# Routed experts on gathered token tiles instead of on every token, in a one-core attention and mixture-of-experts kernel

## The chip, the cores and the metric

The kernel runs on one core of one Trainium2 chip. The metric is device microseconds of one launch; the kernel before takes 1021.36 us (median of 3 runs, 1020.69 to 1021.43).

## What is computed

The input x is 8 sequences of 256 tokens with H = 256 (2048 tokens). A first block (normalised attention with quantised projections, self and cross, 16 heads of 128) adds its output to x. The change touches the second block only:

```python
x = x + tanh(g_ffn[0]) * ffn(_layernorm(x))

def _moe_forward(hidden_states, gate_w, w1, w3, w2, sw1, sw3, sw2):   # T 2048, E 8, I 176, K 2
    scores = softmax(x @ gate_w.T)
    topk_w, topk_idx = top_k(scores, K)
    topk_w = topk_w / sum(topk_w)
    h = einsum('th,ehi->eti', x, w1)
    g = einsum('th,ehi->eti', x, w3)
    y_all = einsum('eti,eih->eth', silu(h) * g, w2)
    y = sum(y_all[topk_idx, tok] * topk_w)
    shared = silu(x @ sw1) * (x @ sw3) @ sw2                          # width 352
    return y + shared
```

## The kernel before, in words

Each engine has its own program, written out by hand, and semaphores join them: `done(engine, s, n)` waits until counter s has passed n. The attention stage is 64 steps (8 sequences by 8 groups) in a software pipeline that is six steps deep; `tick(b, g)` on each engine issues that engine's share of up to six steps. `tick(B, g)` for g = 0 to 4 drains it and already does the first steps of the second block. Step `tick(B, 4)` ends with the last output projection (L456, into the PSUM bank JB). `residual` (L992) adds the last sequence to xs, `tail1` takes its statistics, POOL's `tail` (L1366) normalises it into zf, PE turns it (L337), and ACT and DVE write it as two fp16 halves, `tail_high` (L641) and `tail_low` (L954), into zT_hi and zT_lo. All matrix products of the second block are three matmuls (`split3`, L319: high by high, high by low, low by high).

The second block treats the 8 experts and the shared expert as one hidden width of 1760 for all tokens. It goes over 4 blocks of 512 tokens, and in each over 14 chunks of 128 hidden columns (the last has 96): `ffn_up` (L527) is 2 by 6 matmuls of 512 columns, `ffn_down` (L556) 12 matmuls of 256 columns, and for the 11 chunks of experts `weigh` (L602) spreads the routing weight of each token over the rows by one matmul into the bank VB, so that an expert that a token did not choose counts zero. ACT takes the silu (L870) and the high half (L865), DVE the product (L1302), the weight (L1307) and the sum into the output (`finish`, L1284), and POOL the low half (L1458). The chunks of block 0 are written out and overlap with the rest of the routing, the weights' halves (`ffn_high` on ACT, L660, `ffn_low` on DVE, L986, 7 units of two chunks, each loaded by SP) and the last sequence's normalisation; blocks 1 to 3 run as a loop. The routing itself is `logits` on PE, `read_logits`, `best` and `weights` on DVE (L1238 to L1278), in two portions: the first 14 tiles of 128 tokens, and the last sequence's two.

SP issues the loads, the transposes of the attention (`flip`) and the stores. POOL issues one DMA (wp, L1438). `JB`, `VB`, `A0`, `A1`, `S0`, `S1`, `T0`, `T1` are the 8 PSUM banks; the profile leaves the numbers out.

## Time and profile before

| | |
|---|---|
| median of 3 runs | 1021.36 us |
| the profiled execution's own time | 1020.03 us |
| its span, first to last instruction | 1018.3 us |
| PE busy | 930.3 us (91%), 6752 matmuls |
| DVE, ACT busy | 760.0 us, 759.8 us (75% each) |
| POOL busy | 704.2 us (69%) |
| granted TensorE clock, mean | 0.973 |
| DMA | 63.12 MB, 62 GB/s |
| chain that ended last | PE 59%, issue 16%, DVE 10%, POOL 6%, ACT 5% |

A busy share is of the whole span. Matmuls are pipelined: the time of one in a timeline is longer than the distance to the next, and the distance is what counts where they follow each other. The granted clock is 1.00 at 2.4 GHz and 0.50 at 1.2 GHz.

### The profile page before, as it was taken

The numbers are of one execution on the slowest core, as the hardware profiler recorded it, in microseconds if no ns is written. First come the engines' busy times: TensorE is split into PE (matmuls) and PEld (weight loads), VectorE is DVE, ScalarE is ACT, GpSimd is POOL, SyncE is SP. The second block draws the span as 40 slices with busy tenths as digits, with TensorE's granted clock in tenths as the row PEclk, the third lists the DMA queues.
The fourth block names the chain that finished last, engine by engine and source line by source line (L and its number), as shares of the span: only waits on it lengthen the run. The fifth ranks groups of instructions, "written<-read, shape, count | busy, mean of one in ns | idle before, by whom it ended". The sixth has DMA issues, their size and how long they took to land.

```text
span 1018.3 us, 21021 instructions
## 1 busy us (share of the span) xinstructions
PE 930.3 (91%) x6752; PEld 665.4 (65%) x6752; DVE 760.0 (75%) x1612; ACT 759.8 (75%) x2396; POOL 704.2 (69%) x533
## 2 busy tenths in 40 slices
PE   0375899999999999999999999999976999999998
PEld 0254677778787787778778777877733555555554
DVE  8899789888888988888988889898863833333332
ACT  3486899999999999999999999999873432222221
POOL 4597789799898888979988988888831422232322
PEclk9697899999999999999999999999997999999999
DMA  9323223333242333324233332423434100000000
GB/s 251 104 83 101 61 53 74 58 62 68 51 77 51 68 61 62 67 51 77 51 69 60 59 70 51 77 51 71 112 64 118 59 1 22 1 21 0 21 0 21
DMA packets 183265, 63.12 MB, mean 62 GB/s; under 512 B 167248, under 2 KB 180912, under 8 KB 183232
## 3 DMA queue, kind: packets, MB, share of 16 engines
q1 hardware_dynamic: 179120, 60.62, 27.3%
q0 software_dynamic: 4112, 2.10, 1.5%
q8 instruction: 17, 0.28, 0.1%
q14 instruction: 16, 0.13, 0.0%
HBM read 20.76 MB, written 2.10 MB: 22 GB/s over the span
## 4 chain that ended last, share of the span: by engine, by line
PE 59%; issue 16%; DVE 10%; POOL 6%; ACT 5%; DMA 1%; SPq 1%; POOLq 0%; DVEq 0%; ACTq 0%
PE S L426 10%; PE A L329 7%; PE A L330 7%; PE T L397 5%; POOL pT L1458 5%; PE JB L456 5%; PE S L414 4%; PE VB L321 3%; PE VB L323 2%; PE VB L322 2%; PE T L447 2%; DVE stage L977 1%; ACT zq L637 1%; DVE zq L935 1%; PE T L322 1%
## 5 line engine op out<-in xcount | busy, mean ns | idle before, releaser
L1346 POOL TENSOR_TENSOR rstd<-var,mhalf 128x8 f32<-128x8 f32 (+1 forms) x128 | 191.1, 1509 | 76.7 <-DVE var L1054 76.3
L329 PE MATMUL A<-w_hi,xq 128*128 128x256 f16 (+1 forms) x1024 | 187.4, 249 | 35.4 <-DVE v_lo L1028 20.5
L1458 POOL TENSOR_TENSOR pT<-zq,pT 128x512 f16<-128x512 f32 (+1 forms) x56 | 65.3, 1165 | 181.9 <-ACT pT L865 174.3
L330 PE MATMUL A<-w_lo,xq 128*128 128x256 f16 (+1 forms) x1024 | 187.4, 249 | 0.0
L426 PE MATMUL S<-kT,qT 128*128 128x256 f32 x512 | 142.1, 401 | 8.5 <-ACT kT L732 4.3
L870 ACT ACTIVATE qT<-A 128x512 f32<-128x512 f32 (+1 forms) x56 | 33.4, 596 | 152.2 <-PE A L323 152.2
L1040 DVE TENSOR_SCALAR qT<-T,qmap 128x512 f32<-128x512 f32 x128 | 103.6, 809 | 55.5 <-PE T L397 55.5
L1012 DVE TENSOR_REDUCE nmx<-S 128x2 f32<-128x512 f32 (+1 forms) x192 | 114.7, 598 | 28.0 <-PE S L426 25.6
L329 PEld LDWEIGHTS A<-w_hi,xq 128*128 128x128 f16 x1024 | 101.3, 99 | 47.0 <-issue 30.7
L743 ACT ACTIVATE prob<-S,nmx 128x256 f32<-128x256 f32 x256 | 119.3, 480 | 14.8 <-DVE nmx L1012 13.5
L1408 POOL TENSOR_TENSOR raw<-raw,rstd 128x1024 f32<-128x1024 f32 x64 | 126.3, 1974 | 0.0
L1392 POOL TENSOR_TENSOR prob<-prob,rl 128x1024 f32<-128x1024 f32 x64 | 120.9, 1889 | 0.0
L426 PEld LDWEIGHTS S<-kT,qT 128*128 128x128 f32 x512 | 89.9, 194 | 42.1 <-ACT kT L732 15.1
L330 PEld LDWEIGHTS A<-w_lo,xq 128*128 128x128 f16 x1024 | 101.3, 99 | 7.7
L1302 DVE SCALAR_TENSOR_TENSOR qT<-S,qT 128x512 f32<-128x512 f32 x44 | 30.4, 690 | 95.4 <-PE S L323 90.6
L698 ACT ACTIVATE raw<-A 128x512 f32<-128x512 f32 x128 | 80.1, 626 | 5.1 <-PE A L330 5.1
L751 ACT ACTIVATE probx<-S,nmx 128x64 f32<-128x64 f32 x256 | 77.7, 336 | 7.4 <-DVE nmx L1012 7.4
L1017 DVE SCALAR_TENSOR_TENSOR psrc<-prob,psrc 128x1024 f16<-128x1024 f32 x64 | 77.9, 1217 | 3.8 <-ACT psrc L767 3.8
L397 PE MATMUL T<-idt,raw 128*128 128x128 f32 x512 | 79.3, 278 | 1.0 <-ACT yb L776 1.0
L1045 DVE TENSOR_REDUCE ss<-sq 128x8 f32<-128x1024 f32 x64 | 77.4, 1210 | 0.0
L691 ACT ACTIVATE sq<-A 128x512 f32<-128x512 f32 x128 | 71.2, 627 | 3.2 <-PE A L330 3.2
L456 PE MATMUL JB<-wp,yb 128*128 128x256 f16 x512 | 67.2, 275 | 4.4 <-DVE yb L1075 4.4
(187 smaller groups left out, 2599.4 us busy)
## 6 DMA issues: line engine op xcount, KB each, us to landing
stage<-wallT SPq DMA_DIRECT2D x8, 1024.0 KB, 4.9
wp<-wpT POOLq DMA_DIRECT2D x1, 2048.0 KB, 30.5
out<-v_lo SPq DMA_DIRECT2D x8, 256.0 KB, 2.2
xs<-x SPq DMA_DIRECT2D x1, 1792.0 KB, 20.5
pT<-psrc SPq DMA_TRANSPOSE x64, 4.9
sq<-w2s SPq DMA_DIRECT2D x7, 128.0 KB, 3.1
sq<-w1T SPq DMA_DIRECT2D x3, 256.0 KB, 3.3
sq<-w3T SPq DMA_DIRECT2D x3, 256.0 KB, 3.2
```

The costliest lines, as they stand in the source:

```text
L329: nc.tensor.matmul(o, l, w_hi[:, c, col:col + n], start=(c == 0), stop=False)
L330: last = nc.tensor.matmul(o, l, w_lo[:, c, col:col + n], start=False, stop=(c == HC - 1))
L397: last = nc.tensor.transpose(o[:, h * S + t * P:h * S + (t + 1) * P], raw[:, p, UQ + t * 2 * HPG + k * HPG + h, :], idt[:, :])
L426: last = nc.tensor.matmul(o[:, t * S:(t + 1) * S], qT[:, p, 0, h, t * P:(t + 1) * P], kT[:, p, 0:S], start=True, stop=True)
L456: last = nc.tensor.matmul(JB[:, t * H:(t + 1) * H], cq[:, p, j, t * P:(t + 1) * P], wp[:, row, :], start=(og == 0 and j == 0 and t == 0), ...
L743: last = nc.scalar.activation(prob[:, p, :, j, :], o[:, t * S:(t + 1) * S].rearrange("p (k s) -> p k s", s=P), ACT.Exp, bias=nmx[:, p, j:j ...
L1012: nc.vector.tensor_reduce(nmx[:, p, j:j + rows], o[:, 0:rows * w].rearrange("p (r w) -> p r w", w=w), AX.X, ALU.max, negate=True).then_inc ...
L1040: nc.vector.tensor_scalar(qT[:, p, k, :, :].rearrange("p h s -> p (h s)"), o[:, :], qmap[:, 2 * k:2 * k + 1], qmap[:, 2 * k + 1:2 * k + 2] ...
L1346: return nc.gpsimd.tensor_tensor(dst, src, mhalf[:, 0:n], ALU.pow)
L1392: nc.gpsimd.tensor_tensor(prob[:, p, :, :, :], prob[:, p, :, :, :], rl[:, p, 0:PJ].rearrange("p (o j i) -> p o j i", o=1, i=1).to_broadcas ...
L1408: nc.gpsimd.tensor_tensor(raw[:, p, 0:UK, :], raw[:, p, 0:UK, :], rstd[:, p, 0:UK].rearrange("p (u o) -> p u o", o=1).to_broadcast([P, UK, ...
L1458: nc.gpsimd.tensor_tensor(a_lo[0:n, j % 3, :], act_b[0:n, j % 2, :], a_hi[0:n, j % 3, :], ALU.subtract).then_inc(f_alo, 1)
```

## The change

The routed experts run on the tokens that chose them. Every token's two choices get a rank within their expert: on PE by matmuls of the 0/1 membership (`memb`) with a triangle and with ones (`rank_early` for the first 14 token tiles, `carry_early` and `rank_late` for the last two), on DVE `ranks`. `marks(t)` writes two pairs of 0/1 matrices per token tile (4 instructions), and `table(t)` multiplies them into a table of token numbers by slot. `count_tiles` and `plan_tiles` give each expert as many tiles of 128 slots as it needs; `pick_tokens` and `read_tokens` put the token numbers of 39 tiles (`NTL`, whatever the data is) as columns into `tokidx`, and the expert of each tile into `expert`. The normalised rows of all tokens go to DRAM (`zd`) as they come, by `store_z`.

For each of the 39 tiles POOL gathers 128 rows of 1 KB (`fetch_z`, an indirect DMA, three buffers), PE turns them (`turn_z`, 2 matmuls), ACT and DVE split them (`high_z`, `low_z`), PE reads the tile's expert number into a register (`value_load`, twice a tile) and does `expert_up` (6 matmuls of 352 columns: both w1 and w3) with the weights' address from it, ACT takes the silu (`expert_silu`), DVE the product (`expert_mul`), PE turns it (`turn_a`, 2 matmuls), ACT and DVE split that (`high_a`, `low_a`), PE does `expert_down` (6 matmuls of 256 columns), ACT reads it out (`read_y`), and SP stores it to DRAM (`yd`). The steps of four tiles interleave. Then POOL gathers the two rows of each token back from `yd` (`fetch_y`, 32 indirect DMAs, 16 buffers), and DVE adds them with their weights (`mix`, 4 instructions for each pair of token tiles).

The shared expert has 3 chunks for each of the 4 token blocks. Those of block 0 (`shared_up` in ticks 0 to 2, then `shared_down`) stand ahead of the tiles, the 9 others behind them, and their low halves on POOL stand between the second gathers. The weights come as 5 units instead of 7 (one shared, four of two experts each). `weigh`, the transposed weights and yout are gone.

```diff
+            def store_z(tb):
+                done(sp, ta_z, tb)
+                sp.dma_start(zd[tb * S:(tb + 1) * S, :].rearrange("(t p) h -> p t h", p=P), zf[:, :, :]).then_inc(st_z, 16)
...
+            for j in range(NTL):
+                done(sp, e_y, j)
+                sp.dma_start(yd[j * P:(j + 1) * P, :], yo[:, j % 3, :]).then_inc(st_y[j % 3], 16)
...
+                if n % G == 4 and n > G:
+                    store_z(n // G - 1)
...
-                if live(m, FSTEPS):
-                    ffn_up(blk, j, weights_next=routed(j))
-                    if routed(j):
-                        weigh(blk, j)
-                if live(m - FLAG, FSTEPS):
-                    ffn_down(m - FLAG, (j - FLAG) % FC, blk)
...
+            def table(t):
+                done(pe, f_oh, t)
+                if t == 0:
+                    done(pe, a_core, STEPS - 1)
+                for k in range(2):
+                    last = nc.tensor.matmul(VB[:, R_TAB:R_TAB + P], ring[:, t % NR, k, 1, :], ring[:, t % NR, k, 0, :],
+                                            start=(t == 0 and k == 0), stop=False, skip_group_check=True)
+                last.then_inc(f_tab, 1)
...
+            def turn_z(j):
+                pe.wait_ge(ld_zg[j % 3], 16 * (j // 3 + 1))
+                if j < 2:
+                    done(pe, f_idxr, 0); done(pe, ta_lo, B - 1)
+                done(pe, e_zl, j - 2)
+                for c in range(HC):
+                    last = nc.tensor.transpose((JB, VB)[j % 2][:, c * P:(c + 1) * P], zg[:, j % 3, c * P:(c + 1) * P], idt[:, :])
+                last.then_inc(e_zt, 1)
+
+            def expert_up(j):
+                if j == 0:
+                    done(pe, f_idx, 0)
+                    pe.wait_ge(f_wlo, UNITS)
+                    done(pe, f_a, M0 - 1)
+                e = pe.value_load(expert[0:1, j:j + 1], min_val=0, max_val=E - 1)
+                done(pe, e_zl, j)
+                done(pe, e_a, j - 2)
+                o = (S0, S1)[j % 2][:, 0:2 * I]
+                for c in range(HC):
+                    wh, wl = (w[:, c, bass.ds(e * (2 * I), 2 * I)] for w in (w13_hi, w13_lo))
+                    zh, zl = (zt[:, j % 2, k, c * P:(c + 1) * P] for k in range(2))
+                    last = split3(o, zh, zl, wh, wl, start=(c == 0), stop=(c == HC - 1))
+                last.then_inc(e_up, 1)
+
+            def turn_a(j):
+                done(pe, e_a, j)
+                done(pe, e_al, j - 2)
+                for k in range(2):
+                    last = nc.tensor.transpose((A0, A1)[j % 2][0:HE, k * P:(k + 1) * P], ea[:, j % 2, k * HE:(k + 1) * HE], idt[:, :])
+                last.then_inc(e_at, 1)
+
+            def expert_down(j):
+                e = pe.value_load(expert[0:1, j:j + 1], min_val=0, max_val=E - 1)
+                done(pe, e_al, j)
+                if j < 2:
+                    done(pe, f_fin, M0 // FS - 1)
+                done(pe, e_y, j - 2)
+                o = (T0, T1)[j % 2][:, 0:H]
+                for k in range(2):
+                    wh, wl = (w[:, bass.ds(e * (2 * H) + k * H, H)] for w in (w2_hi, w2_lo))
+                    ah, al = (at[:, j % 2, i, k * P:(k + 1) * P] for i in range(2))
+                    last = split3(o, ah, al, wh, wl, start=(k == 0), stop=(k == 1))
...
+                if g == 2:
+                    rank_early()
+                if g == 3:
+                    for t in range(4): table(t)
+            shared_down(0)
+            for t in range(4, 8): table(t)
+            shared_down(1)
+            for t in range(8, 12): table(t)
+            shared_down(2)
+            done(pe, ta_z, B - 1)
+            transpose_tokens(zf, ta_T, JB)
+            for t in range(12, NE): table(t)
+            carry_early()
+            done(pe, ta_lo, B - 1)
+            logits(NT - ST, NT, VB, R_LG - (NT - ST) * E, False).then_inc(f_lgm, 1)
+            rank_late()
+            for t in range(NE, NT): table(t)
+            pick_tokens()
+            turn_z(0)
+            for j in range(NTL + 2):
+                if j + 1 < NTL: turn_z(j + 1)
+                if j < NTL: expert_up(j)
+                if 0 <= j - 1 < NTL: turn_a(j - 1)
+                if 0 <= j - 2 < NTL: expert_down(j - 2)
+            for m in range(M0, MS):
+                shared_up(m)
+                if m - 2 >= M0: shared_down(m - 2)
+            for m in range(MS - 2, MS): shared_down(m)
 
...
+            ffn_high(2)
+            ffn_high(3)
+            tail_high(B - 1, JB)
+            ffn_high(4)
+            high_z(0)
+            for j in range(NTL + 2):
+                if j + 1 < NTL: high_z(j + 1)
+                if j < NTL: expert_silu(j)
+                if 0 <= j - 1 < NTL: high_a(j - 1)
+                if 0 <= j - 2 < NTL: read_y(j - 2)
+            for m in range(M0, MS):
+                shared_silu(m)
+                if m - 1 >= M0: shared_high(m - 1)
...
+            def marks(t):
+
+                done(dve, f_tab, t - NR)
+                if t == 0:
+                    done(dve, mm_kv, STEPS - 1)
+                for k in range(2):
+                    nc.vector.tensor_scalar(ring[:, t % NR, k, 0, :], kc[:, K_IOTA:K_IOTA + P], rlo[:, t, k:k + 1], None, ALU.is_equal)
+                    last = nc.vector.tensor_scalar(ring[:, t % NR, k, 1, :], kc[:, K_COL:K_COL + P], col[:, t, k:k + 1],
+                                                   kc[:, K_TOK + t:K_TOK + t + 1], ALU.is_equal, ALU.mult)
+                last.then_inc(f_oh, 1)
...
+            def mix(q):
+
+                done(dve, f_fin, 2 * q // BT)
+                dve.wait_ge(ld_yk[q % (NG // 4)], 64 * (q // (NG // 4) + 1))
+                for k in range(2):
+                    for t in (2 * q, 2 * q + 1):
+                        i = 2 * t + k
+                        last = nc.vector.scalar_tensor_tensor(xs[:, t, :], yk[:, i % NG, :], cw[:, k, t:t + 1], xs[:, t, :], ALU.mult, ALU.add)
+                    if k == 0:
+                        last.then_inc(f_out, 1)
+                        done(dve, f_out, q)
+                last.then_inc(f_mix, 1)
...
+            residual(B - 1)
+            tail1(B - 1)
+            for t in range(4, 8): marks(t)
+            ffn_low(2)
+            for t in range(8, 12): marks(t)
+            finish(0)
+            ffn_low(3)
+            for t in range(12, NE): marks(t)
+            tail_low(B - 1, JB)
+            ffn_low(4)
+            read_logits(1, NE, NT, VB, R_LG - NE * E)
+            for k in range(2): best(1, NE, NT, k)
+            members(NE, NT)
+            ranks(1, NE, NT, VB)
+            count_tiles()
+            for t in range(NE, NT): marks(t)
+            plan_tiles()
+            read_table()
+            read_tokens()
+            mix_weights(1, NE, NT)
+            low_z(0)
+            for j in range(NTL + 1):
+                if j + 1 < NTL: low_z(j + 1)
+                if j < NTL: expert_mul(j)
+                if 0 <= j - 1 < NTL: low_a(j - 1)
+                if j == 4: slots()
+            for m in (3, 4): shared_mul(m)
+            mix(0)
+            shared_mul(5)
+            mix(1)
+            shared_mul(6)
+            finish(1)
+            mix(2)
+            shared_mul(7)
...
         @block.gpsimd
@@ -1365,6 +1615,8 @@
 
             def tail(tb):
                 done(pool, ta_var, tb)
+                if not isinstance(tb, int) or tb > 0:
...
+            def fetch_z(j):
+                if j == 0:
+                    done(pool, f_idx, 0)
+                    pool.wait_ge(st_z, 16 * B)
+                done(pool, e_zt, j - 3)
+                pool.indirect_dma_start(zg[:, j % 3, :], None, zd, bass.IndirectOffsetOnAxis(ap=tokidx[:, j:j + 1], axis=0)
+                                        ).then_inc(ld_zg[j % 3], 16)
+
+            def fetch_y(i):
+                if i == 0:
+                    done(pool, f_slot, 0)
+                    for r in range(3):
+                        pool.wait_ge(st_y[r], 16 * len(range(r, NTL, 3)))
+                if i >= NG:
+                    done(pool, f_mix, (i - NG) // 4)
+                pool.indirect_dma_start(yk[:, i % NG, :], None, yd, bass.IndirectOffsetOnAxis(ap=slotidx[:, i:i + 1], axis=0)
...
+            for m in range(3): shared_low(m)
+            tail(B - 1)
+            exps(1, NE, NT)
+            for j in range(NTL): fetch_z(j)
+            shared_low(M0)
+            shared_low(M0 + 1)
+            for i in range(2 * NT):
+                fetch_y(i)
+                if i % 4 == 3 and M0 + 2 + i // 4 < MS: shared_low(M0 + 2 + i // 4)
```

How the order moves, at three places. In the engines' order, names are tiles as the program allocates them: xq is the ring of 0/1 matrices, ctx_lo and ctx_hi the routing's scratch, psrc the gathered rows, prob the activations of a tile.

PE in the steady part of the tiles, from the end of one tile's `expert_down` over `turn_z` into the next `expert_up` (in the kernel before, PE has nothing like it: its step is 12 matmuls 128x512, at most one more, and 12 of 128x256):

```order
L380 MATMUL T<-w_hi,prob 128x256
L683 MATMUL JB<-idt,psrc 128x128 x2
L691 TENSOR_LOAD w_lo
L691 ISA x2
L378 ISA
L378 MATMUL S<-w_hi,psrc 128x352
L379 REGISTER_ALU
L379 MATMUL S<-w_lo,psrc 128x352
L380 MATMUL S<-w_hi,psrc 128x352
```

The three rows from L378 to L380 come once more, and `turn_a` and `expert_down` follow in the same manner with a load of their own: each of a tile's two weight products stands behind a load of a register and arithmetic on it, on PE's own queue.

DVE around the last sequence's residual, before:

```order
L989 SCALAR_TENSOR_TENSOR w_lo<-raw,w_hi 128x2x256 x2
L989 SCALAR_TENSOR_TENSOR w_lo<-raw,w_hi 128x512
L1302 SCALAR_TENSOR_TENSOR qT<-S,qT 128x512
L1307 TENSOR_TENSOR zq<-qT,VB 128x512
L996 SCALAR_TENSOR_TENSOR xs<-JB,gates,xs 128x256 x2
L906 MEMSET hold_cell 128x1
L911 BN_STATS bst<-xs 128x6 x2
```

and now:

```order
L1447 TENSOR_SCALAR xq<-w_lo,ctx_lo 128x128
L1448 TENSOR_SCALAR xq<-w_lo,ctx_lo 128x128
L1206 TENSOR_SCALAR yb<-yb 128x1024
L1211 TENSOR_SCALAR yb<-yb 128x1024
L1132 SCALAR_TENSOR_TENSOR xs<-JB,gates,xs 128x256 x2
L1041 MEMSET hold_cell 128x1
L1046 BN_STATS bst<-xs 128x6 x2
L1041 MEMSET hold_cell 128x1
L1051 BN_AGGR mv<-bst 128x2 x2
L1054 SCALAR_TENSOR_TENSOR ve<-mv,epst 128x2
L1447 TENSOR_SCALAR xq<-w_lo,ctx_lo 128x128
```

The residual no longer stands behind weighted chunks of block 0, but behind ranks and marks (the last two of tick 3's 16 are shown), and marks and a unit's low halves stand behind it.

POOL from the last sequence's normalisation to its end, now (`zd` and `yd` are read by indirect DMAs; before, the loop of L1458 stood here):

```order
L1596 TENSOR_TENSOR rs<-ve,mhalf 128x2
L1600 TENSOR_TENSOR zf<-xs,mv 128x512
L1603 TENSOR_TENSOR zf<-zf,rs 128x512
L1704 TENSOR_TENSOR ctx_hi<-euler,ctx_hi 128x2
L1716 DMA psrc<-zd,w_lo 128x256 x39
L1709 TENSOR_TENSOR pT<-zq,pT 128x512 x2
L1726 DMA wp<-yd,w_lo 128x256 x4
L1709 TENSOR_TENSOR pT<-zq,pT 96x512
L1726 DMA wp<-yd,w_lo 128x256 x4
L1709 TENSOR_TENSOR pT<-zq,pT 128x512
L1726 DMA wp<-yd,w_lo 128x256 x4
```

The gathers of tiles stand behind everything that the routing needs; the gathers back and the low halves of the shared chunks share the queue.

## Rows read from the trace of the kernel before

**Rows 1.** Windows; busy us (instructions) per engine, then granted clock, DMA share, GB/s.

```profile
core 0: us, PE busy (x) PEld busy (x) DVE busy (x) ACT busy (x) POOL busy (x), PEclk, DMA share, GB/s
748.00:790.00 42.00, 29.39 (x150) 14.55 (x150) 20.80 (x49) 19.75 (x45) 9.55 (x7) 0.88 0.37 92
770.00:783.00 13.00, 6.36 (x22) 2.83 (x23) 6.77 (x16) 5.45 (x12) 1.15 (x1) 0.61 0.36 109
953.00:1018.00 65.00, 60.55 (x365) 34.55 (x362) 20.75 (x36) 16.12 (x29) 17.32 (x15) 0.99 0.05 16
```

**Rows 2.** PE timeline, one step of the FFN loop; start us, us, name.

```profile
904.19 0.38 PE L321 MATMUL A<-stage,w_hi 128*128 x1
904.41 0.38 PE L322 MATMUL A<-stage,w_hi 128*128 x1
...
907.20 0.28 PE L572 MATMUL T<-w_hi,pT 128*128 128x256 f16 x1
...
908.52 0.38 PE L321 MATMUL A<-stage,w_hi 128*128 x1
```

**Rows 3.** Groups by line and shape, 829 to 1018 us: busy us, mean ns.

```profile
L1458 POOL TENSOR_TENSOR pT<-zq,pT 128x512 f16<-128x512 f32 x40 | 46.2, 1156 | 124.4 <-ACT pT L865 124.4
```

**Rows 4.** PE timeline, end of the attention stage.

```profile
734.28 0.63 PE L397 MATMUL T<-idt,raw 128*128 128x128 f32 x4 [0.52 <-ACT yb L776]
734.74 1.00 PE L414 MATMUL S<-kT,qT 128*128 128x64 f32 x8
...
772.83 0.61 PE L446 MATMUL T<-pT,vx_hi 128*128 128x512 f16 x1 [4.07 <-ACT yb L776]
...
779.47 0.63 PE L321 MATMUL A<-stage,w_hi 128*128 128x512 f16 x1
...
781.88 0.38 PE L321 MATMUL S<-stage,w_hi 128*128 128x512 f16 x1
...
786.64 1.05 PE L456 MATMUL JB<-wp,yb 128*128 128x256 f16 x8
```

**Rows 5.** DVE timeline, 735 to 835 us.

```profile
772.08 1.90 DVE L989 SCALAR_TENSOR_TENSOR w_lo<-sq,w_hi 128x512 f16<-128x512 f32 x3 [7.54 <-ACT w_hi L663]
...
776.28 0.22 DVE L1276 CAST raw<-sq 128x112 f16<-128x112 f32 x1
...
793.86 0.87 DVE L996 SCALAR_TENSOR_TENSOR xs<-JB,gates,xs 128x256 f32<-128x256 f32 x2
...
810.36 0.17 DVE L1254 TENSOR_REDUCE raw<-sq 128x2 f32<-128x16 f32 x1
...
812.64 0.16 DVE L1262 TENSOR_TENSOR raw<-raw 128x2 f32<-128x2 f32 x1
...
817.46 1.03 DVE L1277 CAST sq<-raw 128x16 f32<-128x16 f16 x1
```

**Rows 6.** ACT timeline, same stretch.

```profile
770.38 1.67 ACT L663 ACTIVATE w_hi<-sq 128x512 f16<-128x512 f32 x3 [6.17 <-DMA sq<-w2s]
...
774.38 0.86 ACT L776 ACTIVATE yb<-T,rsm 128x256 bf16<-128x256 f32 x2
```

**Rows 7.** POOL timeline, start of the program.

```profile
1.25 1.89 POOL L1438 DMA_DIRECT2D wp<-wpT  x1 [0.79 <-POOLq L1509]
```

**Rows 8.** POOL timeline, 735 to 835 us.

```profile
796.21 0.69 POOL L1346 TENSOR_TENSOR rs<-ve,mhalf 128x2 f32<-128x2 f32 x1
...
798.06 1.30 POOL L1353 TENSOR_TENSOR zf<-zf,rs 128x512 f32<-128x512 f32 x1
...
817.31 1.15 POOL L1458 TENSOR_TENSOR pT<-zq,pT 128x512 f16<-128x512 f32 x1 [2.51 <-ACT pT L865]
```

**Rows 9.** Groups by line and shape of the whole span, ACT and DVE.

```profile
L743 ACT ACTIVATE prob<-S,nmx 128x256 f32<-128x256 f32 x256 | 119.3, 480 | 14.8 <-DVE nmx L1012 13.5
L1028 DVE SCALAR_TENSOR_TENSOR v_lo<-A,vscale,v_hi 128x256 f16<-128x256 f32 x64 | 30.3, 473 | 0.0
```

**Rows 10.** DMA issues: KB each, median us from issue to landing.

```profile
out<-v_lo SPq DMA_DIRECT2D x8, 256.0 KB, 2.2
```

More of the change, by code:

```diff
@@ L1105, in tick @@
                         low_px(n0 - 3, par(3))
-                        ffn_tick(0, 0)
-                        best(0, 0, NT - ST, 1)
+                        shared_mul(0)
+                        best(0, 0, NE, 1)
+                        members(0, NE)
                         ffn_low(1)
@@ L1343, in _ @@
+            mix(2)
+            shared_mul(7)
+            mix(3)
+            for m in (8, 9): shared_mul(m)
+            finish(2)
+            mix(4)
+            shared_mul(10)
+            mix(5)
+            shared_mul(11)
+            finish(3)
+            for q in range(6, NT // 2): mix(q)
         @block.gpsimd
```

644 lines of the change are left out of this document (348 added, 296 removed).

## The prediction

> **What bounds the kernel now.** I read the windows first. From 748 to 790 us, where the attention drains, PE is busy 29.39 of 42 us at a granted clock of 0.88; from 953 to 1018 us 60.55 of 65 us at 0.99 [rows 1]: the FFN is a stage in which PE never waits. The PE timeline shows its step: from 904.19 to 908.52, 4.33 us, with 12 matmuls of 512 columns 0.22 us apart, one of the weights, and 12 of 256 columns in 1.32 us, 0.11 each [rows 2]. The group of POOL's low half, 1.16 us [rows 3], and everything else fit beside that. The chain of the page calls much of this "issue"; it is PE's queue of matmuls. 44 of the 56 steps are for experts, 44 x 4.33 = 190 us, and three quarters of that work is for experts that the token did not choose. So the change attacks what bounds, and the question is what its replacement costs: it is no longer a plain queue of matmuls.
>
> **The new work of PE.** A tile has 6 matmuls of 352 columns, 6 x 0.22 x 352/512 = 0.90 us; 6 of 256, 0.66; and 4 turns of 128 columns, which take 734.28 to 734.74, 0.46 us [rows 4]. That is 2.02 us, 79 us for 39 tiles against 190. ACT has three readings of 256 columns at up to 0.48 us and a shorter silu, some 1.8 us; DVE two of 0.47 and a shorter one, 1.3 us [rows 9]. Both are below 2.02, and the order gives every hand-over about one tile's time, so they hide. 111 us of matmuls go, but five things lie on the path that did not before. I lay them end to end, from the last sequence's residual, because all that stands before it in the attention is the same (store_z adds 7 stores of 256 KB to SP's queue, each issued after its data is there, where the DMA share is 0.37 [rows 1]: nothing; were a transpose held up by each, 7 x 2.2 us at most).
>
> **1. Start.** The residual ends at 793.86 + 0.87 = 794.7 us [rows 5]. Two things held it: ACT waited 6.17 us for a unit's load and spent 1.67 on it before its last scalings, the last at 774.38 [rows 6], and DVE had chunks and a unit in front. Now units 2 to 4 stand behind the ticks. ACT's last scaling moves from 775.2 up by 7.8 to 767.4; I allow 2.9 for PE's product before it, 770.3. But DVE first does ranks (8 instructions of up to 420 columns, 2.6 us) and 16 marks; a mark is nearest to the 128x112 cast of 0.22 us [rows 5], 0.19 where nothing is waited for, 3.1 us. They end at 773.4. Clip and round 0.9, the last projection 1.05 [rows 4], residual 0.87, with hand-overs: 776.5, 18 us earlier.
>
> **2. DVE's queue behind it.** Statistics 1.3; 40 marks, 7.6; three units of 1408 + 1024 columns, where 1536 take 1.90 [rows 5], 3.0 each, 9.0; finish of block 0, four of 0.48, 1.9; tail_low 0.7; 1.7 of waits for PE: 22.2, to 798.7. Beside it POOL normalises in 0.69 + 1.04 + 1.30 [rows 8] and PE turns and multiplies; both are done before.
>
> **3. The last two token tiles' routing.** Nothing overlaps here, since every instruction reads the one before. From 810.36 to 812.80 the trace has 13 such instructions, 0.19 each [rows 5]. The change has 50 in a row up to the token numbers (1 read, 13 of best, 1 of members, 8 of ranks, 1 count, 8 marks, 15 of plan_tiles, 3 reads): 10.0, and three passes to PE and back 1.2. To 809.9. PE is idle in nearly all of it.
>
> **4. First gather.** No indirect DMA is in the trace. POOL's one DMA took 1.89 us to issue, for 2 MB [rows 7]. Bounds for the issue of one gather of 128 rows: 0.7 us (rs, POOL's shortest instruction there [rows 8]) and 1.9. It has far fewer pieces than wp, but must read its indices: I take 1.2. Landing 2.2 us, as the stores [rows 10], then turn and two readings, 1.2: 814.5.
>
> **5. The tiles.** 39 tiles and 2 steps to fill and drain, at a period T. Not below 2.02. What I do not see in the trace is the register load and the arithmetic before each product, two groups a tile. If PE's queue takes them while earlier matmuls run, they cost nothing; if each stands alone, their price is that of an exchange with memory, of which the trace has the 2.2 us landing as the far end, 2.02 + 2 x 2.2 = 6.4; one half of it each way and half covered is 1.1 and T = 3.1 to 4.2. The first two matmuls behind a load wait for nothing else and 0.66 to 0.90 us of work is queued at that time, so I take most as covered, nearest to the near end: T = 2.8. 41 x 2.8 = 114.8, to 929.3. Gathers fit: 1.2 of issue a tile, and three buffers give 8.4 us for 1.2 + 2.2. The Trainium skill ("DMA: Bandwidth & Descriptors", Latency and other measured facts) gives a register load a floor of about 600 ns; uncovered, an estimate of 2.02 + 1.2 = 3.2 a tile and 16 us more in sum; no row here shows one.
>
> **6. Turnover.** The first gather back waits for all 39 stores (2.2 us after the last), but also stands behind the low halves of shared chunks 3 and 4: two ups of 12 x 0.22, 5.2, then silu, product, high, low of 0.6, 0.7, 0.6, 1.16 [rows 3], less 1.2 that begins before the last tile ends: 7.1, to 936.4.
>
> **7. POOL's queue.** 32 gathers at 1.2 and 7 low halves at 1.16 [rows 3], 46.5, to 982.9. PE's nine shared steps, 9 x (2.64 + 1.32) = 35.6, and DVE's 32 additions of 0.48 hide beside it: POOL is the engine that sets the end.
>
> **8. Close.** Landing 2.2, the last pair's four additions 1.9, store 0.5 + 2.2: 989.7.
>
> **Sum.** 776.5 + 22.2 + 11.2 + 4.6 + 114.8 + 7.1 + 46.5 + 6.8 = 989.7 us of span, against 1018.3: 28.6 less. The profiled execution took 1020.03, 1.7 more than its span, and the median shown, 1021.36, is 1.3 above that. So 1021.36 - 28.6 = **992.8 us**, 2.8% less. The sum moves by 41 us for each us of T and by 32 for each us of a gather's issue; it breaks even at T = 3.5, or at a gather of 2.1 us.
>
> **Rivals.**
> *The register loads stand alone.* PE's queue is in order, so a wait in front of a load keeps the load from running ahead: in each tile the turn waits for DVE, and the load stands behind it. At 1.1 us each T = 2.02 + 2.2 = 4.2, 41 x 1.4 = 57 us more, 1050 us, slower. It decides from 0.75 us per load. For it: 12 register instructions a tile that nothing before has. Against: blocks 1 to 3 of the FFN also take their addresses from registers, and PE shows no gap [rows 2]. 0.18.
> *The clock falls in the tiles.* After an idle of 4.07 us PE's 512-column matmuls take 0.61 instead of 0.38 us, still so at 779.47, and are back at 781.88 [rows 4]; the granted clock of 770 to 783 is 0.61 [rows 1]. If waits in the tiles keep it at the lower level of 1.2 GHz, T = 4.0 or more: 49 us more, 1042. Against: at that level PE would be busy nearly all the time, as in the windows where it is granted 1.00. 0.07.
> *Gathers are dear.* At 817.46 us a cast of 16 columns takes 1.03 us, where other DVE instructions of that size take 0.17, and POOL's 1.15 runs from 817.31 beside it [rows 5, 8]: DVE and POOL hold each other up over SBUF. If each gather back waits for one of DVE's additions of 0.48, 32 x 0.5 = 16 us more, 1009; at wp's 1.89, 22 more, 1015. The Trainium skill ("SBUF — State Buffer", Who interferes with whom) has such a lock, and descriptors of POOL's DMAs that wait for it, for DVE's fast copies; the trace agrees for the small cast. In the tiles DVE reads PSUM, so only the end would pay. 0.15.
> *All is covered.* T = 2.2 and gathers of 1.0: 25 + 6 less, 962. For it: the depth of the order. 0.18.
> That the change doesn't take the matmuls out can't be: the count of 39 tiles stands in the code. That leaves 0.42 for the forecast.
>
> **Numbers.** Range: 950 (all covered, and the routing 10 us shorter) to 1040, which leaves out most of the first rival, and the far end of step 5, T = 6.4, altogether. About 0.2% is what a measurement of this kernel can tell from no change; 1019 to 1023 lies between cases. Faster: 0.42, 0.18, 0.15 less a little, that is 0.70; same 0.03; slower 0.27.
>
> **What would show it.** PE's up matmuls for the first tile near 814 us, each of the 39 about 2.8 apart, granted clock over 0.9 there; the last near 920; a POOL queue without gaps to about 983, its groups 4 x 1.2 + 1.16. Wrong: a PE that waits at the first matmul behind each load (first rival), for the gathers (`ld_zg`), or for `f_wlo`; POOL with gaps at the end, so that PE or DVE sets it; a first tile later than 825.

## The result, and the profile after

| | before | after |
|---|---|---|
| median of the runs, us | 1021.03 (1020.26 to 1021.43) | 1032.56 (1031.5 to 1033.8) |
| span of the profiled execution, us | 1018.3 | 1031.0 |
| mean granted clock of PE | 0.973 | 0.933 |

The ratio is 1.0114, with a 95% interval of 1.0097 to 1.0132: slower by 11.5 us, where 992.8 and faster was forecast. 28.6 us were to go; instead 11.5 were added. The sum missed by 1031.0 - 989.7 = 41.3 us of span. The page's summary already shows that the end is no longer PE's queue:

```profile
PE 853.4 (83%) x6339; PEld 630.6 (61%) x6339; DVE 776.1 (75%) x1748; ACT 758.4 (74%) x2450; POOL 721.3 (70%) x560
...
PE   0475899999999999999999999999775367778653
...
PEclk9687999999999999999999999999896589999876
```

The first row is each engine's busy time; the other two are PE's busy tenths and its granted clock in 40 slices of 25.8 us. Before, PE was busy for 60.55 of the 65 us from 953 on, at a clock of 0.99 [rows 1]; now slices 29 to 40 read 7 7 5 3 6 7 7 7 8 6 5 3, and the clock drops in two places: the gap of the routing, and the last stage. The same as windows:

```profile
core 0: us, PE busy (x) PEld busy (x) DVE busy (x) ACT busy (x) POOL busy (x), PEclk, DMA share, GB/s
748.00:790.00 42.00, 28.37 (x143) 14.83 (x143) 25.86 (x71) 22.49 (x47) 12.42 (x8) 0.83 0.44 103
790.00:826.00 36.00, 12.73 (x103) 7.69 (x100) 31.09 (x105) 2.80 (x3) 3.51 (x4) 0.55 0.13 38
860.00:900.00 40.00, 30.71 (x212) 20.19 (x210) 14.86 (x40) 16.88 (x54) 12.29 (x13) 1.00 0.29 89
950.00:990.00 40.00, 25.83 (x124) 13.62 (x122) 10.03 (x21) 6.58 (x12) 16.77 (x17) 0.89 0.20 61
990.00:1031.00 41.00, 18.89 (x88) 10.55 (x85) 14.52 (x32) 3.48 (x6) 24.17 (x25) 0.67 0.31 96
```

In the tiles (860 to 900) PE is busy 30.71 of 40 us at a clock of 1.00; in the routing 12.73 of 36 at 0.55; in the last 81 us 44.72 of 81. The three stretches lie in steps 5, 3 and 7 of the sum.

**The last stage.** POOL's timeline from the last tile on (start, duration, what it did, and the idle time before it):

```profile
956.20 1.15 POOL L1709 TENSOR_TENSOR pT<-zq,pT 128x512 f16<-128x512 f32 x1 [1.43 <-ACT pT L801]
957.50 0.96 POOL L1726 DMA_INDIRECT wp<-yd,w_lo  x1
...
961.27 0.95 POOL L1726 DMA_INDIRECT wp<-yd,w_lo  x1 [0.30 <-issue]
967.21 1.15 POOL L1709 TENSOR_TENSOR pT<-zq,pT 96x512 f16<-96x512 f32 x1 [4.99 <-ACT pT L801]
968.51 0.95 POOL L1726 DMA_INDIRECT wp<-yd,w_lo  x1
...
978.23 1.15 POOL L1709 TENSOR_TENSOR pT<-zq,pT 128x512 f16<-128x512 f32 x1 [5.00 <-ACT pT L801]
...
989.25 1.16 POOL L1709 TENSOR_TENSOR pT<-zq,pT 128x512 f16<-128x512 f32 x1 [5.01 <-ACT pT L801]
...
1000.32 1.15 POOL L1709 TENSOR_TENSOR pT<-zq,pT 96x512 f16<-96x512 f32 x1 [5.06 <-ACT pT L801]
...
1023.68 0.94 POOL L1726 DMA_INDIRECT wp<-yd,w_lo  x1 [0.30 <-issue]
```

Behind four gathers POOL stands idle for 4.99, 5.00, 5.01 and 5.06 us, each time in front of a low half (L1709, the rows named pT), waiting for ACT. The gathers themselves are 0.95 us with 0.30 between them, a pitch of 1.25 us, as forecast (1.2). DVE and ACT show who holds ACT up:

```profile
964.07 1.80 DVE L1526 SCALAR_TENSOR_TENSOR xs<-wp,ctx_lo,xs 128x256 f32<-128x256 f32 x4 [9.61 <-DMA wp<-yd,w_lo]
965.79 0.68 DVE L1507 SCALAR_TENSOR_TENSOR zq<-S,qT 96x512 f32<-96x512 f32 x1
```

and ACT behind them:

```profile
966.50 0.63 ACT L801 ACTIVATE pT<-zq 96x512 f16<-96x512 f32 x1 [7.00 <-DVE zq L1507]
```

The first row of DVE is mix(0): it waited 9.61 us for the gathers into yk (named wp). The second is shared_mul(5), which stands behind it in DVE's queue though its inputs are long there; then ACT's high half at 966.50, and POOL's low half at 967.21. So POOL, DVE and ACT, with the DMA between them, go round in lockstep: four gathers, their landing, the mix, the product, the high half, the low half, and only then the next four gathers. A round takes 11.0 us (967.21 to 978.23) where POOL has work for 6.2.

**The tiles.** PE's timeline of one tile:

```profile
880.26 0.32 PE L378 MATMUL S<-w_hi,psrc 128*128 x1 [0.36 <-issue]
...
881.16 0.38 PE L705 MATMUL A<-idt,prob 128*88 128x128 f32 x2
881.90 0.28 PE L378 MATMUL T<-w_hi,prob 88*128 x1 [0.35 <-issue]
...
882.56 0.38 PE L683 MATMUL VB<-idt,psrc 128*128 128x128 f32 x2
883.28 0.32 PE L378 MATMUL S<-w_hi,psrc 128*128 x1 [0.34 <-issue]
```

A tile takes 883.28 - 880.26 = 3.02 us (the gathers that follow the tiles' turns, from 849.89 to 922.45, give 3.02 over 24 tiles as well). PE waits for no engine there, but twice a tile it stands 0.35 us in front of the first matmul whose address comes from a register, put down to "issue".

**The start.** The attention is no longer than before up to 732 us (the projection of 1.04 us stands at 730.66, before at 731.46), and then loses. ACT's conversion of unit 0:

```profile
740.71 2.29 ACT L788 ACTIVATE w_hi<-sq 128x704 f16<-128x704 f32 x4 [7.37 <-DMA sq<-s]
```

and in the kernel before:

```profile
738.49 1.67 ACT L663 ACTIVATE w_hi<-sq 128x512 f16<-128x512 f32 x3 [4.36 <-DMA sq<-w2s]
```

PE's pv_core(63), the product of probabilities and values of the last step, now and before:

```profile
773.93 0.61 PE L378 MATMUL VB<-pT,v_hi 128*128 128x512 f16 x1 [3.06 <-DMA pT<-psrc]
```

```profile
767.29 0.39 PE L321 MATMUL VB<-pT,v_hi 128*128 128x512 f16 x1 [0.85 <-DMA pT<-psrc]
```

and the last projection, for which the last residual waits:

```profile
786.68 1.89 PE L513 MATMUL JB<-wp,yb 128*128 128x256 f16 x8 [0.40 <-DVE yb L1211]
```

DVE's timeline: a rounding, shared_mul(2), the first instruction of ranks, the last clip, the last residual:

```profile
769.63 0.43 DVE L1211 TENSOR_SCALAR yb<-yb 128x1024 uint16<-128x1024 uint16 x1
778.04 0.69 DVE L1507 SCALAR_TENSOR_TENSOR zq<-S,qT 96x512 f32<-96x512 f32 x1 [7.98 <-POOL pT L1709]
778.64 0.44 DVE L1427 TENSOR_TENSOR ctx_hi<-ctx_hi,T 128x112 f32<-128x112 f32 x2
...
785.74 0.42 DVE L1206 TENSOR_SCALAR yb<-yb 128x1024 f16<-128x1024 bf16 x1
...
788.61 0.88 DVE L1132 SCALAR_TENSOR_TENSOR xs<-JB,gates,xs 128x256 f32<-128x256 f32 x2 [1.99 <-PE JB L513]
```

ACT waits 7.37 us for unit 0 (the shared expert's weights), before 4.36; pv_core(63) waits 3.06 us for its transposition, and runs at 773.93 where it ran at 767.29 before; DVE stands idle for 7.98 us in front of shared_mul(2); then come 7.1 us of ranks and marks, and only behind them the clip (785.74) that the last projection waits for. That projection runs at half clock, 1.89 us where it took 1.05 before [rows 4].

### The profile page after: what moved, and what is told of

Its sections match the earlier page's. It is cut to its first block, busy times and chain, and to the rows that moved or that the text cites. A ratio compares the mean times of both kernels' runs of the same rounds, so it can differ in the third digit from the quotient of the medians.

```text
span 1031.0 us, 20898 instructions
## 1 busy us (share of the span) xinstructions
PE 853.4 (83%) x6339; PEld 630.6 (61%) x6339; DVE 776.1 (75%) x1748; ACT 758.4 (74%) x2450; POOL 721.3 (70%) x560
## 4 chain that ended last, share of the span: by engine, by line
PE 64%; DVE 14%; issue 7%; ACT 6%; DMA 4%; POOL 4%; SPq 1%; POOLq 0%; DVEq 0%; ACTq 0%
PE S L483 10%; PE A L386 7%; PE A L387 7%; PE T L454 5%; PE JB L513 4%; PE S L471 4%; PE VB L378 3%; PE T L378 3%; PE VB L380 2%; PE VB L379 2%; PE T L380 2%; PE T L379 2%; PE S L378 2%; PE T L504 2%; DMA wp<-yd,w_lo 2%
## 5 line engine op out<-in xcount | busy, mean ns | idle before, releaser
L1148 DVE TENSOR_REDUCE nmx<-S 128x2 f32<-128x512 f32 (+1 forms) x192 | 114.8, 598 | 27.4 <-PE S L483 25.2
L386 PEld LDWEIGHTS A<-w_hi,xq 128*128 128x128 f16 x1024 | 101.5, 99 | 47.5 <-issue 30.9
L1716 POOL DMA_INDIRECT psrc<-zd,w_lo x39 | 37.0, 949 | 77.5 <-PE VB L683 34.4
L471 PE MATMUL S<-kT,qT 128*128 128x64 f32 x512 | 67.6, 275 | 1.1 <-ACT prob L880 1.1
L904 ACT ACTIVATE psrc<-prob 128x1024 f16<-128x1024 f32 x64 | 67.8, 1059 | 0.0
```

Of the source, the lines that this page charges most:

```text
L386: nc.tensor.matmul(o, l, w_hi[:, c, col:col + n], start=(c == 0), stop=False)
L471: last = nc.tensor.matmul(S0[:, k * SC:(k + 1) * SC], qT[:, p, 1, h, t * P:(t + 1) * P], kT[:, p, S:KT], start=True, stop=True)
L1148: nc.vector.tensor_reduce(nmx[:, p, j:j + rows], o[:, 0:rows * w].rearrange("p (r w) -> p r w", w=w), AX.X, ALU.max, negate=True).then_inc ...
```

## The experiments

Each kernel is the kernel after with the edit shown; ratios are to the kernel before, timed beside it (medians of 1020.4 to 1020.6 us). Differences in us are to the kernel after, 1032.56, which was not timed again beside them, so differences of 1 us say nothing.

**a1_mix_behind: is the last stage a lockstep?**

```
-            for m in (3, 4): shared_mul(m)
-            mix(0)
-            shared_mul(5)
-            mix(1)
-            shared_mul(6)
+            for m in (3, 4, 5, 6): shared_mul(m)
+            mix(0)
+            shared_mul(7)
             finish(1)
+            mix(1)
+            shared_mul(8)
             mix(2)
...
```

> The kernel after, with one edit on DVE: each mix(q) stands one shared multiplication later, so that shared_mul(m) no longer waits for the gather that is issued ahead of shared_low(m) on POOL. THEORY LOCKSTEP: in the tail of the kernel after, POOL stands idle 4.99, 5.00, 5.01 and 5.06 us in front of shared_low(5) to (8), since the low half waits for ACT's high half, that for DVE's product, and that stands on DVE behind mix(q), which waits for the four gathers that POOL has just issued. With the mix later the queue on POOL closes up to the 46.5 us that were predicted: 20 us less, 1012 us (1009 to 1016). RIVAL PE: the nine shared steps on PE (35.6 us of work) run at the lower clock there and set the pace once the waits are gone: 1018 to 1024. RIVAL LANDING: the gathers themselves are late (ring of 16 buffers, landing of 2 us or more) and POOL would wait for mix(q) instead: over 1025.

Measured: 1013.69 us, ratio to before 0.9936 (0.9919 to 0.9953); 18.9 less than the kernel after. POOL's queue there:

```profile
956.65 0.95 POOL L1725 DMA_INDIRECT wp<-yd,w_lo  x1
...
960.42 0.95 POOL L1725 DMA_INDIRECT wp<-yd,w_lo  x1 [0.30 <-issue]
961.38 1.17 POOL L1708 TENSOR_TENSOR pT<-zq,pT 96x512 f16<-96x512 f32 x1
962.71 0.95 POOL L1725 DMA_INDIRECT wp<-yd,w_lo  x1 [0.16 <-issue]
...
1003.53 0.95 POOL L1725 DMA_INDIRECT wp<-yd,w_lo  x1 [0.30 <-issue]
```

No gap over 0.31 us is left; from the first gather to the end of the last it is 1004.48 - 956.65 = 47.8 us, for 46.5 forecast. The order of DVE's queue alone turns the sign: with it the kernel is 0.64% faster than the one before. The edit moves the first four mixes behind two more products, not one as the expectation says, the next two behind one, and two of the closing sums behind one; whether less is enough was not tried. RIVAL PE falls: PE waits for POOL there, up to 2.1 us. RIVAL LANDING falls too, since no gather stands behind a gap of more than 0.31 us.

**a2_const_expert: what do the register loads cost?** The experts' outputs are those of the constant expert j modulo 8, so this kernel computes something else in the tiles.

```
-                e = pe.value_load(expert[0:1, j:j + 1], min_val=0, max_val=E - 1)
+                e = j % E
```

> The kernel after, but TensorE takes the expert of tile j as the constant j modulo 8 in place of loading it into a register twice a tile; the experts' results are therefore those of other weights. Everything else, the gathers too, is as in the kernel after. THEORY: a tile takes 3.03 us in the kernel after, of which PE is busy some 2.3 and stands 0.35 us twice, in front of the first matmul of expert_up and of expert_down (put down to issue); those are the register loads. Without them PE sets a period of 2.3 to 2.4, 39 x 0.65 = 25 us less: 1007 us (1003 to 1011). RIVAL CHAIN: the hand-overs among ACT, DVE and PE bound a tile at close to 3 us anyway, and the loads only lie in their shadow: less than 8 us, 1025 to 1032. RIVAL GATHER: POOL's gathers (issued only when the reading of three tiles earlier is done) bound it at 2.7 or so: 1020.

Measured: 995.11 us, 0.9754 (0.9738 to 0.9770); 37.4 less, beyond the theory's range. The tile:

```profile
869.90 0.31 PE L378 MATMUL S<-w_hi,psrc 128*128 128x352 f16 x1
...
871.67 0.38 PE L683 MATMUL JB<-idt,psrc 128*128 128x128 f32 x2
871.89 0.31 PE L378 MATMUL S<-w_hi,psrc 128*128 128x352 f16 x1
```

and the window of 850 to 880 us (PE, PEld, DVE, ACT, POOL busy, clock, DMA share, GB/s):

```profile
850.00:880.00 30.00, 30.00 (x244) 24.41 (x242) 17.07 (x46) 18.99 (x61) 14.18 (x15) 1.00 0.44 133
```

1.99 us a tile, and PE busy 30.00 of 30: the 2.02 us of matmuls that were forecast, and no hand-over, gather or other engine limits it. The two loads of a tile, with the arithmetic on the register that gives the weights' addresses and that goes with them here, cost 3.02 - 1.99 = 1.03 us, not the 0.7 of the two gaps: the profile models the ends of matmuls, and its gaps show less than the time lost. Both rivals fall.

**b1_one_load, b2_loads_in_fours, c1_two_together, c2_load_at_down: where does a load cost?**

```
             def expert_down(j):
-                e = pe.value_load(expert[0:1, j:j + 1], min_val=0, max_val=E - 1)
+                e = experts.pop(j)
```

In b1 expert_up keeps what it loads; in b2 it loads four in a row at every fourth tile; in c1 two next to each other; in c2 the one load of a tile (the expert of the next expert_up) stands in front of expert_down.

> The kernel after, with the expert's number loaded into a register once a tile (for expert_up) and kept for expert_down two tiles later, in place of twice. With no load at all (a2_const_expert) a tile took 1.99 us in place of 3.03, so the two loads cost 1.04 us. THEORY STAND-ALONE: each load stops PE for the same 0.52 us, wherever it stands: the period becomes 2.51 us, 39 x 0.52 = 20 us less, 1012 us (1009 to 1015). RIVAL ONE OF THEM: only the load in front of expert_up costs (or the one in front of expert_down), the other lies under matmuls that are still running: under 5 us less or over 35.

> As b1_one_load, but the experts of four tiles are loaded in a row, in front of every fourth expert_up. THEORY STAND-ALONE: a load costs 0.52 us each, so four in a row 2.1 us: the time is that of b1_one_load within 3 us. RIVAL DRAIN: the cost is mostly that of emptying PE's queue and filling it again, the loads of a row overlap: four cost 0.8 us or so, and the time is 10 to 14 us under that of b1_one_load (998 to 1002).

> The kernel after, with both register loads of a tile next to each other in front of expert_up; expert_down uses the second one two tiles later. Measured so far: no load 1.99 us a tile, one (in front of expert_up) 2.14, two apart 3.03, and four in a row once in four tiles 2.40 (4 x 0.41). THEORY RUN-AHEAD: PE's sequencer runs ahead of the matrix unit and takes some 0.9 us over a load (3.03 - 2.14), so that one load a tile hides in the 2 us of matmuls and a second doesn't, wherever it stands: the period stays near 3.0 us and the time within 6 us of the kernel after's 1032.5 (1026 to 1034). RIVAL PLACE: it is the load in front of expert_down that costs (0.89 us), since it stands behind turn_a's wait with only two transpositions queued ahead of it, and the one in front of expert_up costs 0.15: then two in front of expert_up cost at most 2 x 0.41 = 0.8, the period is 2.3 to 2.8 and the time 1005 to 1023.

> The kernel after with one register load a tile, and that in front of expert_down (it fetches the expert of the next expert_up, and is kept for its expert_down). THEORY RUN-AHEAD: one load a tile hides under the matmuls wherever it stands: 2.1 to 2.2 us a tile, the time of b1_one_load (1001.5) within 4 us. RIVAL PLACE: the load in front of expert_down costs 0.89 us: 2.9 us a tile, 1024 to 1032.

| kernel | loads per tile | us a tile | median us | ratio to before (95%) |
|---|---|---|---|---|
| after | 2, apart | 3.02 | 1032.56 | 1.0114 (1.0097 to 1.0132) |
| c1 | 2, together | 2.80 | 1025.45 | 1.0048 (1.0032 to 1.0065) |
| b2 | 4 each fourth tile | 2.41 | 1013.53 | 0.9928 (0.9911 to 0.9945) |
| b1 | 1, in front of expert_up | 2.15 | 1001.46 | 0.9811 (0.9794 to 0.9829) |
| c2 | 1, in front of expert_down | 2.15 | 1000.75 | 0.9807 (0.9790 to 0.9823) |
| a2 | none | 1.99 | 995.11 | 0.9754 (0.9738 to 0.9770) |

The times a tile are those of 24 tiles in the middle of the stage, by the pitch of their gathers. STAND-ALONE falls at b1: one load costs 0.16 us (the arithmetic on its register included), the second 0.87. The rival of b1 misses as well: 31.1 us less lies between its "under 5" and "over 35". RIVAL PLACE falls at c2: in front of expert_down one load costs the same 0.16. So a load is mostly hidden when it is the only one among 2 us of matmuls, and a second one is not. c1 lies just outside both ranges (1026 to 1034 for RUN-AHEAD, 1005 to 1023 for PLACE, 1025.45 measured), and its period of 2.80 is not RUN-AHEAD's "near 3.0": together the two cost 0.81, apart 1.03, so the place counts for 0.2 us. b2, where four loads follow each other, pays 0.42 for each and loses 12 us against b1, where its theory had the same time and its rival 998 to 1002: neither held, and bunching the loads undoes the cover. That fits a sequencer that works ahead of the matrix unit by a bounded amount and takes some 0.9 us over a load; the profile has no rows for it, so the mechanism is inferred from these six periods, and only the periods are shown.

**a3_ranks_ahead: DVE's idle time at the start.**

```
                         whole_out(n0 - 5, par(5))
-                        shared_mul(2)
                         ranks(0, 0, NE, T0)
                         for t in range(4): marks(t)
+                        shared_mul(2)
```

> The kernel after, with the early ranks and the first sixteen marks ahead of shared_mul(2) on DVE in place of behind it. DVE stands idle from 770.06 to 778.04 us there, and the moved work is 7.1 us. THEORY: this idle time takes the work up, the last clip comes at about 778.6 in place of 785.74, and all that follows on DVE up to the routing comes 7 us earlier: 1025.5 us (1024 to 1027). RIVAL: the clip comes earlier, but what follows waits for others (TensorE at half clock for the last projection and the shared downs, ACT's high halves of units 2 to 4): 2 to 4 us, 1029 to 1031. RIVAL NOTHING: DVE's idle time isn't open to it, since the counting matmuls on PE come too late: 1032.

Measured: 1027.12 us, 1.0067 (1.0050 to 1.0084); 5.4 less. DVE:

```profile
771.04 0.45 DVE L1427 TENSOR_TENSOR ctx_hi<-ctx_hi,T 128x112 f32<-128x112 f32 x2 [0.85 <-PE T L641]
...
779.74 0.40 DVE L1206 TENSOR_SCALAR yb<-yb 128x1024 f16<-128x1024 bf16 x1
...
782.59 0.88 DVE L1132 SCALAR_TENSOR_TENSOR xs<-JB,gates,xs 128x256 f32<-128x256 f32 x2 [1.98 <-PE JB L513]
```

The ranks start at 771.04 in place of 778.64, the clip at 779.74 in place of 785.74, the residual 6.0 us earlier. It is 1.6 us less than the theory's 7: ranks now wait 0.85 us for the counting on PE; what follows kept nearly all of the 6.0.

**a4_loads_behind and d1_store_behind: why is unit 0 late?**

```
             flip(STEPS - 4)
-            store_z(B - 2)
-            sp.wait_ge(mm_kT, STEPS - 1)
-            load_up(1)
...
             sp.wait_ge(d_ss, STEPS)
             load_shared(True)
             flip(STEPS - 3)
+            store_z(B - 2)
+            sp.wait_ge(mm_kT, STEPS - 1)
+            load_up(1)
...
```

a4 moves the store, the load of unit 1 and the two constants behind the last loads of unit 0 and a transposition; d1 the store alone.

> The kernel after, with the store of the normalised rows, the first load of unit 1 and the constants behind the loads of unit 0 and one transposition on the SP queue, so that unit 0 lands with less beside it. In the kernel after ACT waits 7.37 us for unit 0, before the change 4.36. THEORY: unit 0 lands late because 1.1 MB of other transfers were issued within the same 3 us; with them behind it the wait falls to about 5, and the whole runs 2 to 3 us sooner: 1030 us (1029 to 1031). RIVAL SHAPE: the load itself is slow (rows of 1408 bytes of the shared weights, 1.05 MB in place of 0.75), so the wait stays above 6.5 and the time 1032. RIVAL SHIFT: unit 0 is sooner, but unit 1 then lands too late and takes its place: 1032 to 1035.

> The kernel after, with only the seventh store of normalised rows (256 KB) behind the next transposition on the SP queue; the load of unit 1 and the constants stay ahead of the loads of unit 0. a4_loads_behind moved all three: ACT's wait for unit 0 fell from 7.37 to 2.56 us, and the time by 4.1. THEORY BYTES: each transfer ahead delays unit 0 by its share of the bytes; the store is 256 KB of some 1.23 MB, a fifth: the wait falls by 1 us, to 6.4, the time to 1031.5 (1030.5 to 1032.5). RIVAL STORE: the store is what unit 0 waits for (a write among reads): the wait falls below 4, the time to 1029. RIVAL ORDER: the 704 KB load of unit 1 holds it all, and the store costs nothing: the wait stays over 7, 1032.5.

Measured: a4 1028.43 us, 1.0077 (1.0055 to 1.0099), 4.1 less; d1 1031.75, 1.0098 (1.0079 to 1.0118), which can't be told from the kernel after. ACT's conversion of unit 0 in a4:

```profile
735.43 2.30 ACT L788 ACTIVATE w_hi<-sq 128x704 f16<-128x704 f32 x4 [2.56 <-DMA sq<-s]
```

and in d1:

```profile
739.87 2.29 ACT L788 ACTIVATE w_hi<-sq 128x704 f16<-128x704 f32 x4 [6.11 <-DMA sq<-s]
```

The wait is 7.37 us in the kernel after, 6.11 with the store moved, 2.56 with all three moved. The rows of SP's queue show two parts in it. The last issue for unit 0 in the kernel after, before and in a4:

```profile
735.11 0.46 SPq L323 DMA_DIRECT2D sq<-s  x1
```

```profile
735.04 0.90 SPq L284 DMA_DIRECT2D sq<-w2s  x2
```

```profile
732.57 0.48 SPq L323 DMA_DIRECT2D sq<-s  x1
```

From the end of that issue to ACT's start it is 2.4 us in a4, 2.5 in the kernel before, 4.4 in d1 and 5.1 in the kernel after, with nothing, 556, 980 and 1236 KB of other transfers issued just ahead: that part falls with these bytes. The store, a fifth of them, is a quarter of the gain. The other 2.5 us by which a4 is sooner come from its earlier issue, ahead of the rest in SP's queue. RIVAL SHAPE falls (the same load lands within 2.4 us), RIVAL STORE and ORDER fall, and unit 1 still lands in time. The theory of a4, a wait of about 5 and 1029 to 1031 us, was short of the gain. At the last clip a4 is 6.1 us ahead (779.68), as much as a3; the median shows 4.1 of it, with runs from 1026.05 to 1029.60.

**b3_low_on_dve: the low halves off POOL.**

```
-            shared_low(M0)
-            shared_low(M0 + 1)
             for i in range(2 * NT):
                 fetch_y(i)
-                if i % 4 == 3 and M0 + 2 + i // 4 < MS: shared_low(M0 + 2 + i // 4)
```

On DVE each shared_mul(m) is followed by the low half of m - 1, and the mixes stand as in a1.

> The kernel after, with the low halves of the nine shared steps behind the tiles on DVE in place of POOL, each mix(q) behind the next shared multiplication. POOL's queue there is then the 32 gathers alone. THEORY: the first of them no longer stands behind two low halves (957.5 becomes about 951.5), the waits of 20 us go, and 32 x 1.255 = 40.2 us are left in place of 67.1: 1032.5 - 6 - 27 = 999.5 us (997 to 1003). RIVAL DVE: mixes (8 x 1.8), three closing sums (5.0), nine products (6.2) and nine low halves (4 to 6) are 31 us on DVE, but in a chain with PE and ACT: DVE or PE's nine steps set the end, 1003 to 1010.

Measured: 1001.63 us, 0.9818 (0.9801 to 0.9834); 30.9 less. POOL:

```profile
950.44 0.94 POOL L1742 DMA_INDIRECT wp<-yd,w_lo  x1 [18.88 <-DMA yd<-psrc]
...
991.69 0.94 POOL L1742 DMA_INDIRECT wp<-yd,w_lo  x1 [0.30 <-issue]
```

The first gather waits for the last store of the tiles' outputs alone, and the 32 take 42.2 us (theory 40.2): single ones take up to 1.69 us there (968.57), in c3 up to 1.67, while DVE does the low halves and the mixes. Why was not tried. The time lies in the theory's range, 1.4 us below that of RIVAL DVE; PE waits twice for low halves on DVE near the end (2.1 and 3.2 us).

**b4_combined and c3_combined_low_on_dve.** b4 is a1, a3, a4 and b1 together; c3 is b4 with b3 in place of a1.

> The kernel after with four edits together: the mix one step later (a1, 19 us), the ranks ahead (a3, 5.4 us), the loads behind (a4, 4.1 us), one register load a tile (20 us expected). THEORY: the parts lie one behind the other and add up, except that a3 fills an idle time which a4 leaves as it is: 1032.5 - 48.5 = 984 us (981 to 989), 3.5% under the kernel before. RIVAL: they overlap (the start's two edits move the same wait; faster tiles make the gathers bound the tile stage): 990 to 998.

> b4_combined (970.3) with the low halves of the nine shared steps behind the tiles on DVE in place of POOL. THEORY: as b3 stands to a1 (1001.6 to 1013.7), 12 us less: 958.3 us (956 to 962); POOL's queue is the 32 gathers alone, 40.2 us. RIVAL: with the tiles sooner and the clock as before, PE's nine steps set the pace of the products and closing sums: 962 to 968.

Measured: b4 970.29 us, 0.9507 (0.9491 to 0.9522); c3 958.14, 0.9389 (0.9373 to 0.9404). The theory for b4 stood on a load of 0.52 us; with the 31.1 of b1 the four edits come to 18.9 + 5.4 + 4.1 + 31.1 = 59.5, that is 973.1, and 970.3 was measured: they lie end to end and add up to within 2.8 us. c3, 12.2 under b4, is what was expected (958.3). It is 6.1% under the kernel before, and the computation is the whole one.

## Why the prediction was wrong

The direction was wrong, and the time by 39.8 us. That 1032.56 lies inside the stated range (950 to 1040) is no merit: the range was drawn so wide for slow tiles, and the tiles were not what made it slow. Laid beside the eight steps:

| step | forecast us | measured us | difference |
|---|---|---|---|
| 1 start, to the last residual | 776.5 | 789.5 | +13.0 |
| 2 DVE's queue behind it | 22.2 | 25.1 | +2.9 |
| 3 routing of the last two | 11.2 | 11.5 | +0.3 |
| 4 first gather | 4.6 | 5.5 | +0.9 |
| 5 tiles | 114.8 | 116.7 | +1.9 |
| 6 turnover | 7.1 | 9.2 | +2.1 |
| 7 POOL's queue | 46.5 | 67.1 | +20.6 |
| 8 close | 6.8 | 6.4 | -0.4 |

Borders in the trace of after: 789.5, 814.6, 826.1, 831.6 (first product of the tiles), 948.3 (last one), 957.5, 1024.6, 1031.0.

**Step 7 failed, and it decides the sign.** "32 gathers at 1.2 and 7 low halves at 1.16", 46.5 in sum, treats POOL's queue as work without waits, and "POOL is the engine that sets the end" was argued by comparing sums of busy time: 46.5 against PE's 35.6. Both sums were right (a1 has 47.8), but no sum bounds a ring of waits. POOL waits through ACT for DVE, and DVE's queue has the mix, which waits for POOL, ahead of the product. To see it one writes down the two queues side by side, shared_low(5) behind fetch 0 to 3 on POOL, shared_mul(5) behind mix(0) on DVE, and follows one round. No rival of mine had this, though "POOL with gaps at the end" was named as a sign of being wrong, and so was "a first tile later than 825" (it came at 831.6). Without these 20 us the kernel is faster than before, by 0.64% (a1).

**Step 1 failed for two reasons.** That "all that stands before it in the attention is the same" is one: unit 0 has 1056 KB in place of 768, and 1236 KB were issued ahead of its last part in the same 3 us, where before they were 556; that is 4.0 us at 755 us (pv_core(61) at 755.03, before at 751.02): 2.2 for ACT's later start on unit 0 and 0.6 for its longer conversion, the rest because PE, after 6.87 us of idle time, comes back at half clock (four matmuls of 256 columns in 2.07 us for 1.13). Then 0.9 for the larger unit 1 on DVE ahead of the last low half, and 1.7 for a slower transposition (landing 6.7 us after its input in place of 5.0). a4 and d1 show the first part. The stores themselves were put at nothing, and that nearly holds: six of them are issued before 732 us, where the kernel is 0.8 us ahead of the one before, and moving the seventh brings the last clip forward by 0.3 us (785.40, d1). The other reason is the wait that I took for none: 773.4 for the end of the marks asks for ranks that begin at 767.7, which step 1 does not say (from its 770.3 on, 2.6 and 3.1 us would end at 776.0), while DVE stood until 778.04 in front of shared_mul(2), which needs a low half that POOL may write only when the last pv_core is done (776.75), since both use the same buffer. The ranks' own time, 7.1 us for 5.7, is a mark of 0.226 us for 0.19 and ranks of 3.5 for 2.6. a3 shows that the idle time was usable. In b4, which has both edits, the last clip stands at 774.79 and the residual ends at 777.93, 1.4 us behind the forecast. Another 0.8 us of step 1 are the last projection at half clock.

**Steps 2, 3, 4, 6 and 8** held within 3 us. In step 2 the marks are again 0.226 us, 40 of them 1.4 more, and finish(0) waits 3.05 us for PE in place of the 1.7 for all waits: after the waits of the start PE has half its clock, and the 12 matmuls of that product stand 0.21 us apart, in [rows 2] 0.11. In step 3, 50 times 0.19 is 9.5 and not 10.0; 11.5 was measured with the passes to PE. Step 6 counted 1.2 us of overlap with the last tile that isn't there.

**Step 5** was mis-sized in its reason but not in its sum: T is 3.02 for 2.8, but the steps that fill and drain the stage have one load or none, and it lasts 38.6 of them, not 41. Two errors cancel there: that 116.7 us is so near 114.8 is luck. The first rival, that "the register loads stand alone" at 1.1 us each and T = 4.2, did not come; the price from which it was said to decide, 0.75 us, is above the 0.52 measured for each of two. What step 5 held against it (work queued ahead covers the load) fits one load a tile and not two. The Trainium skill ("DMA: Bandwidth & Descriptors", Latency and other measured facts) gives a register load a floor of about 600 ns, by which T = 3.2 was estimated; the traces have 3.02 for two loads a tile and 2.15 for one, 0.16 us over none, so that figure is not what a load costs PE here.

**The other rivals.** The clock did fall, but not in the tiles (1.00 from 860 us on): it fell at the end of the attention (0.83 from 748 to 790), in the routing (0.55) and in the lockstep (0.89 and 0.67), where the waits were. What it cost there, estimated from the distances of the matmuls at either level, is 1.2 us at 745, 1.3 at pv_core(63), 0.8 at the last projection and 1.3 in front of finish(0); in the lockstep POOL does not wait for PE. "Gathers are dear" is out in this kernel: 1.25 us each. "All is covered" is what a2 shows for T, 1.99. So the forecast had the large gain right, 190 us of experts' matmuls become 79 and even take 117 with the loads, and lost it at two places where engines wait for each other: steps 7 and 1 make 33.6 of the 41.3 us.

## What to carry to other kernels

Where two engines' queues refer to each other, the sum of each engine's work bounds nothing: write both queues in order, and follow one round; if a round is longer than the longest engine's share of it, move the consumer of the slow transfer back in its queue. Idle time in front of a wait can take up work that stands behind it (6.0 of 7.1 us in a3): ask of each added piece whether it could run there. And of loads that a change makes larger, count what else is issued in the same few microseconds: with 1.2 MB just ahead, unit 0's last part landed within 5.1 us, with none within 2.4.
